# A gated cross-attention and quantised feed-forward kernel: another start, another steady order, five PSUM banks at the end, and first transposes in halves

## What is computed

```
x1  = x + tanh(g_x) * ((ctx @ Wv) @ Wout + bout)
h   = layernorm(layernorm(x1)) * ln1_g + ln1_b
h   = gelu(quant(h) @ ternary(w1).T + b1)             # 256 -> 1024
h   = layernorm(h) * ln2_g + ln2_b
out = x1 + tanh(g_f) * (quant(h) @ ternary(w2).T + b2)  # 1024 -> 256
quant(h)   = round(h * s) / s,  s = 127 / max|h| of the token
ternary(w) = clip(round(w / mean|w|), -1, 1) * mean|w|
```

## Time and profile before

| | |
|---|---|
| median of three runs | 415.7 us |
| profiled execution | 413.45 us |
| its span, first to last instruction | 411.7 us |
| PE, DVE, ACT, POOL busy | 315.3, 299.3, 274.2, 268.2 us |
| mean granted TensorE clock | 0.893 of full |
| bytes moved | 51.56 MB |

### The profile page before, as it was taken

One profiled execution on the slowest core, in us unless ns is written; L12 is line 12 of the kernel. 1 busy time (PEld: TensorE's weight loads), 2 busy tenths in 40 slices (PEclk: granted clock), 3 DMA queues, 4 the chain that ended last, 5 costly groups with the idle time before them and its releaser, 6 DMA issues. The chain is left out here.

```text
span 411.7 us, 5770 instructions
## 1 busy us (share of the span) xinstructions
PE 315.3 (77%) x1661; PEld 201.2 (49%) x1690; DVE 299.3 (73%) x520; ACT 274.2 (67%) x443; POOL 268.2 (65%) x298
## 2 busy tenths in 40 slices
PE   2976827759798989797979797989897666665553
PEld 2855516343556565555555554656464434332232
DVE  0168395978788989797979798979798858565710
ACT  2113672666878887878787888969695959594220
POOL 4052669386878887878787888787777868484100
PEclk9998987997989998989999999989898969695785
DMA  7665213325385756566665657490707161715173
GB/s 236 240 247 191 61 49 83 102 50 130 83 176 121 184 124 158 139 144 139 144 151 131 160 123 178 106 201 28 154 27 153 53 127 52 129 52 103 62 127 94
DMA packets 97974, 51.56 MB, mean 125 GB/s; under 512 B 86567, under 2 KB 88800, under 8 KB 97942
## 3 DMA queue, kind: packets, MB, share of 16 engines
q1 hardware_dynamic: 97046, 51.14, 50.6%
q10 hardware_dynamic: 896, 0.04, 0.1%
HBM read 21.78 MB, written 8.41 MB: 73 GB/s over the span
## 5 line engine op out<-in xcount | busy, mean ns | idle before, releaser
L343 POOL TENSOR_TENSOR y<-u,g_bc 128x1024 f32<-128x1024 f32 x64 | 151.4, 2368 | 41.5 <-ACT u L512 40.9
L681 DVE TENSOR_TENSOR y<-y,slot_c 128x1024 f32<-128x1024 f32 x64 | 77.8, 1216 | 47.3 <-PE slot_c L929 31.5
L968 PE MATMUL bank_f<-w2T,q2T 128*128 128x256 f16 x512 | 78.8, 308 | 9.9 <-DMA q2T<-q 7.6
L685 DVE TENSOR_REDUCE amax<-y 128x1 f32<-128x1024 f32 x64 | 77.6, 1213 | 1.8
L493 ACT ACTIVATE q<-y,scale 128x1024 f16<-128x1024 f32 x64 | 69.9, 1142 | 12.8 <-DMA q2T<-q 9.7
L520 ACT ACTIVATE junk<-u,usum 128x1024 bf16<-128x1024 f32 x64 | 73.5, 1149 | 2.1
L968 PEld LDWEIGHTS bank_f<-w2T,q2T 128*128 128x128 f16 x512 | 55.7, 109 | 29.9 <-issue 10.2
L512 ACT ACTIVATE u<-slot_a,d 128x1024 f32<-128x1024 f32 x32 | 35.4, 1107 | 38.3 <-PE slot_a L957 38.3
L929 PE MATMUL slot_c<-ln_rows,rows 128*128 128x512 bf16 x112 | 41.7, 447 | 16.2 <-ACT rows L503 8.9
L904 PE MATMUL slot_a<-wvo,ctxT 128*128 128x256 f32 x208 | 51.4, 380 | 0.0
L726 DVE SCALAR_TENSOR_TENSOR res<-bank_f,d,x 128x256 f32<-128x256 f32 x64 | 27.8, 476 | 19.2 <-PE bank_f L971 19.2
(11 more groups left out here) (113 smaller groups left out, 449.6 us busy)
## 6 DMA issues: line engine op xcount, KB each, us to landing
c_in<-in_ctx SPq DMA_DIRECT2D x16, 512.0 KB, 5.0
x_in<-in_x SPq DMA_DIRECT2D x16, 512.0 KB, 3.5
out<-res SPq DMA_DIRECT2D x32, 256.0 KB, 2.0
y<-in_L_ffn_w SPq DMA_DIRECT2D x2, 1024.0 KB, 9.1
u<-in_L_xattn_Wkv SPq DMA_DIRECT2D x2, 512.0 KB, 6.2
u<-in_L_xattn_Wout SPq DMA_DIRECT2D x2, 512.0 KB, 7.5
q2T<-q SPq DMA_TRANSPOSE x64, 3.3
g_bc<-in_L_ffn_ln_g SPq DMA_DIRECT2D x1, 512.0 KB, 4.5
```

What stands on the lines that cost most here:

```text
L343: nc.gpsimd.tensor_tensor(y[:, k % 3, t, :], u[:, t, :], g2_bc[:, :], ALU.mult).then_inc(gain2_done, 1)
L681: nc.vector.tensor_tensor(line, line, slot_c[:, :], ALU.add).then_inc(y_done, 1)
L685: nc.vector.tensor_reduce(amax[:, 1, t:t + 1], y[:, k % 3, t, :], AX.X, ALU.max, apply_absolute_value=True).then_inc(amax2_done, 1)
L968: nc.tensor.matmul(acc, q2T[:, t, j, :], w2T[:, j, :], start=(j == 0), stop=False)
```

## The change

The order of the work changes on all engines, and some of the work changes its engine. No tile gets another shape, apart from the transfers named here.

- Start. The attention of set 0 goes to slot_b, that of sets 1 and 2 to bank_q and bank_f. ACT copies wvo before the second half of context 0. DVE sums w1 before the first residual; both raw weights are rounded by ACT in one instruction (`round_weights`); DVE clamps after the copies to f16 instead (`clamp_first`, `clamp_second`; the copy of w2 clamps from above). w2 is summed and scaled in bodies -1 and 0, and its turns stand between the hidden products of set 0. Both halves of attention 1 come in body -2. SP's first loads and turns are written out one by one.
- Steady order. PE: second product 2 of set i-3 goes ahead of the rows, second product 3 to between correction 0 and hidden 0, correction t+1 behind hidden t, second product 0 between correction 2 and hidden 2, second product 1 between the two halves of the attention; one context turn goes to the end of the body before, the other behind hidden 3. ACT makes three quantisations ahead of the GELUs, and the fourth and a context copy behind them. DVE takes finals 2 and 3 right behind row 0. SP issues the transpose of tile 3, then the first transposes, then those of tiles 0 and 1, and puts the context load, the transpose of tile 2 and a store at the end of the body.
- End. `product_bank` gives the second products of sets 14 and 15 places in bank_q, slot_a and slot_b beside bank_f; a product's bias is a function of its own (`second_bias`); bodies 16 and 17 are written out, body 18 is gone; all transposes of sets 14 and 15 stand before the last stores, the last two of which hold one tile each; the scales of set 15 are made for three tiles and for one.
- First transposes. `turn_first` issues two DMA transposes of two tiles each (128 x 512), with semaphores of their own; `hidden(0)` and `hidden(2)` wait for one each, and q1_done counts pairs of tiles.
- d12 gets three buffers instead of two.

The core of the diff:

```diff
@@ SP @@
             def turn_first(k):
 
-                wait(sp, q1_done, k + 1)
-                wait(sp, hid_done, T * k)
-                sp.dma_start_transpose(q1T[:, :, :], q1[:, :, :].rearrange("p t d -> p (t d)")) \
-                    .then_inc(q1T_in, 16)
+                for h in range(2):
+                    two = slice(2 * h, 2 * h + 2)
+                    wait(sp, q1_done, 2 * k + h + 1)
+                    wait(sp, hid_done, T * (k - 1) + 2 * h + 2)
+                    sp.dma_start_transpose(q1T[:, two.start * KD:two.stop * KD, :],
+                                           q1[:, two, :].rearrange("p t d -> p (t d)")) \
+                        .then_inc(q1T_in[h], 16)
...
+            for i in range(2, S):
                 if live(i - 3):
-                    store(i - 3, 0)
-                    turn_second(i - 3, 2)
                     turn_second(i - 3, 3)
                 if live(i):
                     turn_first(i)
...
                 if live(i - 2):
                     turn_second(i - 2, 0)
+                if live(i + 4):
+                    load_x(i + 4)
+                if live(i - 2):
                     turn_second(i - 2, 1)
                 if live(i - 3):
                     store(i - 3, 1)
+                if live(i + 5):
+                    load_context(i + 5)
+                if live(i - 2):
+                    turn_second(i - 2, 2)
+                    store(i - 2, 0)
...
+            turn_second(S - 3, 3)
+            for t in range(T):
+                turn_second(S - 2, t)
+            for t in range(T):
+                turn_second(S - 1, t)
+            store(S - 3, 1)
+            store(S - 2, 0)
+            store(S - 2, 1)
+            store(S - 1, 0)
+            store_tile(S - 1, 2)
+            store_tile(S - 1, 3)
@@ shared @@
+        def product_bank(k, t):
+
+            half = slice(D * (t % 2), D * (t % 2 + 1))
+            if k < S - 2:
+                return bank_f[:, half]
+            if k == S - 2:
+                return bank_q[:, half] if t < 2 else slot_a[:, half]
+            return (slot_a[:, 512:512 + D], slot_a[:, 512 + D:1024], slot_b[:, 0:D],
+                    slot_b[:, 512:512 + D])[t]
@@ ACT @@
+            def round_weights(w):
+
+                line = (w1_raw, w2_raw)[w][:, :, :].rearrange("p k n -> p (k n)")
+                act.wait_ge(wscaled, w + 1)
+                nc.scalar.activation(line, line, ACT.Copy, bias=ROUND, scale=wscale[:, w:w + 1]) \
+                    .then_inc(wrounded, 1)
...
+                if live(i + 3):
+                    take_context(i + 3, 0)
+                if i <= S:
                     take_rows()
                 if live(i - 2):
                     quantise(i - 2, 0)
                     quantise(i - 2, 1)
+                    quantise(i - 2, 2)
...
                     take_context(i + 3, 1)
...
                 if live(i - 2):
-                    quantise(i - 2, 2)
                     quantise(i - 2, 3)
@@ DVE @@
+            def clamp_first(n):
+
+                dve.wait_ge(w1T_copied, n + 1)
+                nc.vector.tensor_scalar(w1T[:, n, :], w1T[:, n, :], 1.0, -1.0, ALU.min, ALU.max) \
+                    .then_inc(w1T_clamped, 1)
...
+                if i == S:
+                    for t in range(T):
+                        row(S - 1, t)
+                        row_max(S - 1, t)
+                        if t == 2:
+                            scales(slice(1, 2), slice(0, 3))
+                    scales(slice(1, 2), slice(3, 4))
+                    final(S - 3, 2)
+                    final(S - 3, 3)
+                    for t in range(T):
+                        final(S - 2, t)
+                    for t in range(T):
+                        final(S - 1, t)
@@ PE, steady order @@
-                if live(i + 3):
-                    turn_context(i + 3, 0)
+                if live(i - 3):
+                    second_product(i - 3, 2)
+                    second_bias(i - 3, 2)
                 if i <= S + 1:
                     turn_rows()
                 if live(i - 1):
                     correction(i - 1, 0)
-                if live(i + 3):
-                    turn_context(i + 3, 1)
                 if live(i - 3):
-                    second_product(i - 3, 2)
+                    second_product(i - 3, 3)
+                    second_bias(i - 3, 3)
+                if live(i):
+                    hidden(0)
                 if live(i - 1):
                     correction(i - 1, 1)
                 if live(i):
-                    hidden(0)
+                    hidden(1)
                 if live(i - 1):
                     correction(i - 1, 2)
+                if live(i - 2):
+                    second_product(i - 2, 0)
+                    second_bias(i - 2, 0)
                 if live(i):
-                    hidden(1)
-                if live(i - 3):
-                    second_product(i - 3, 3)
+                    hidden(2)
                 if live(i - 1):
                     correction(i - 1, 3)
                 if live(i):
-                    hidden(2)
                     hidden(3)
+                if live(i + 3):
+                    turn_context(i + 3, 1)
                 if live(i + 1):
                     shift_first(i + 1)
-                if live(i - 2):
-                    second_product(i - 2, 0)
-                    second_product(i - 2, 1)
                 if live(i + 3):
                     attention(i + 3, 0)
+                if live(i - 2):
+                    second_product(i - 2, 1)
+                    second_bias(i - 2, 1)
+                if live(i + 3):
                     attention(i + 3, 1)
+                if live(i + 4):
+                    turn_context(i + 4, 0)
```

More of the change, by code:

```diff
@@ L522, in square @@
                         .then_inc(square_done, 1)
+                if i == S:
+                    quantise(S - 2, 0)
+                    quantise(S - 2, 1)
+                    take_rows()
+                    quantise(S - 2, 2)
+                    quantise(S - 2, 3)
+                    for t in range(T):
+                        quantise(S - 1, t)
+                    return
+                if i == S + 1:
+                    take_rows()
+                    return
                 if i == -3:
@@ L531, in body @@
                     take_rows()
+                    weight_copy(1)
                     take_context(2, 0)
                     take_context(2, 1)
-                    nc.scalar.activation(table[:, :], half_neg[:, 0, 0:1], ACT.Gelu)
+                    return
+                if i == 0:
+                    for t in range(T):
+                        quantise_first(0, t)
+                    take_rows()
+                    round_weights(1)
+                    for t in range(T):
+                        gelu(t)
+                        square(t)
+                    return
+                if i == 1:
+                    take_context(3, 0)
+                    for t in range(T):
+                        quantise_first(1, t)
+                    take_context(3, 1)
+                    take_rows()
+                    take_context(4, 0)
+                    for t in range(T):
+                        gelu(t)
+                        square(t)
+                    take_context(4, 1)
                     return
@@ L801, in body @@
                 if live(i - 1):
+                    row_max(i - 1, 0)
+                    row(i - 1, 1)
+                    row_max(i - 1, 1)
+                if i == S:
+                    scales(slice(1, 2), slice(0, 2))
+                if live(i - 1):
+                    row(i - 1, 2)
+                    row_max(i - 1, 2)
                     row(i - 1, 3)
```

243 lines of the change are left out of this document (141 added, 102 removed).

## The result

The changed kernel takes 365.34 us (median of four runs, 364.51 to 365.44) against 415.81 (four runs, 414.34 to 417.16): 0.878 of the time, interval 0.875 to 0.8815. The profiled execution took 364.51 with a span of 362.7. The forecast was 373.0, 7.7 more, with 362 to 391 as its range.

The account below looks back on a forecast made before the run. It took one loop per set, from variance through rows and hidden 0 to the GELUs, as the bound, no engine being full. Start -15.2, middle -14.4 and end -13.1 sum to -42.7, from the 415.7 median to 373 us, range 362 to 391.

Parts of the forecast that it names:

- The loop from rows to GELU 0: Steady sets: one loop per set from variance through rows and hidden 0 to the GELUs, no engine full.
- the lower bound: Steady set without a stall: rows at 5.1 and hidden 0 ready at 8.1 us after the variance, 18.1 us a set.
- If power does the same, the scales end at 3.2 instead of 2.35: Steady sets: DVE's scales stall under POOL's power as seen under a multiply, making a set 18.8 us, not 18.1.
- rival (a): Steady sets: no stall beside the power, 18.1 us per set, 8 us less, 365 in all; chance 0.17.
- ran beside nothing before: Steady sets: in the old order DVE's scales overlapped no POOL work; now they start near 1.5 us after the variance.
- Rival (b): Middle: clock drops in most sets or half transposes land late, about 1.2 us a set, 389 in all; chance 0.22.
- I take the whole's values: Split q1T transposes: each half priced like a whole one, 1.28 us to issue and 3.3 to land.
- a tie, no cost: Split q1T transposes: first half lands by 7.4 us after the variance, near when hidden 0 wants it in an 18.8 set.
- -15.2: Start: set 2's first GELU at 83 us against 98.25, by reordered w1 and w2 preparation and earlier attention.
- Rival (d): Start: the lead isn't kept, 8 of the 15 us are lost, 381 in all; chance 0.10.
- -13.1: End: set 15's first GELU to the end takes 39.6 us against 52.7, with transposes before stores and five banks.
- (c): Middle: second product 3 ahead of hidden 0 waits for a late transpose, 22.3 us a set, 418 in all; chance 0.07.

Follow-up runs that it names:

- The probe: Changed kernel plus two unused DVE operations per steady body, 8 columns under POOL's multiply and 512 beside its power: 377.98 us.
- the late-w2 run: Changed kernel with w2's turns behind set 0's hidden products and w2's sum, scale and rounding also later: 372.63 us.
- the run on the kernel before: Kernel before the change, four transposes of each first context half issued twice from set 4 on: 406.28 us against 415.14, ratio 0.978.
- hidden 0 first: Changed kernel, steady bodies: hidden 0 ahead of second product 3, scales ahead of finals 0 and 1, first-half store behind first transposes, among other moves: 369.71 us, ratio 0.890.
- the scales first: Changed kernel with DVE's scales ahead of finals 0 and 1 in the steady bodies: 368.42 us, ratio 0.887.
- The run with the store between: Changed kernel with the store of set 13's second half ahead of set 15's four transposes on SP: 366.58 us.
- the run with both steps: Changed kernel with w2's turns behind set 0's hidden products and 10 useless matmuls in each of bodies 13 to 15: 358.21 us, ratio 0.8635.

## Why the prediction was right, and where it was off

**The bound.** The loop from rows to GELU 0 was the right one to reckon by: with rows at r 5.07, correction 0, second product 3 and hidden 0 put GELU 0 at 8.10, as the lower bound had it (5.1 and 8.1). ACT's three quantisations end there too, where 8.3 was reckoned: the row of GELU 0 shows no wait for PE.

**The steady order.** What failed is one term: "If power does the same, the scales end at 3.2 instead of 2.35". They ended at r 2.27. From the earlier trace rows a stall beside a multiply was carried over to the power, and 18.8 was taken over 18.1; 18.19 was measured, so rival (a), given 0.17, is what the chip did, and its 365 is the time that was measured. Eleven periods of 0.61 less are 6.7 us, all of the miss in the spans. That the total still lay within the range owes something to the range, which had been drawn to hold (a).

The trace of the kernel before already had the answer. The forecast says that the scales "ran beside nothing before". That is so in the set of the earlier trace rows, where they end at 229.22, as the power starts. It isn't so in the sets at 147, 248 and 267 us. POOL first, then DVE:

```profile
147.71 1.67 POOL L326 TENSOR_TENSOR rstd<-var,half_neg 128x8 f32<-128x8 f32 x1
...
147.78 0.15 DVE L707 TENSOR_TENSOR d<-amax_g,deq 128x8 f32<-128x8 f32 x1
```

An operation with two inputs in SBUF starts 0.07 us into the power and takes 0.15 us, and the two behind it, still beside the power, 0.17 and 0.16. This was a row nearer in kind than the earlier trace rows. The probe shows both halves: beside the multiply an 8-column operation is held to its end, beside the power even a 512-column one is not. The rule of the Trainium skill's page "SBUF — State Buffer" (Who interferes with whom), that such pairs exclude each other for the whole instruction, agrees with the multiply here (0.75 us, and 2.12 and 2.21 in the late-w2 run) and not with the power (0.12 to 0.17, and 0.68). By the measurement it must not be used for this power. Why the power lets DVE through, no run tells.

**The clock.** Full clock in the middle was forecast and came (1.00 over the 11 periods with attention, 0.97 over all 13). Rival (b) did not occur. What the clock is worth was not split off in the forecast; the run on the kernel before puts it at 0.70 of the 1.79 per set. In the last passages half clock was forecast, with 19.8 for the first two; 20.05 came, and the run with 10 useless matmuls shows that the clock is the whole of their difference to 18.0.

**DVE nearly the bound.** Forecast 17.6 busy with gaps; 17.39 of 18.08 was seen. It is why hidden 0 first gained nothing; the scales first lost by the transpose of tile 3.

**The halves.** "I take the whole's values": right for the issue (1.22 against 1.28), too long for the landing (2.5 against 3.3). It made no difference, as forecast ("a tie, no cost"); with one whole transfer the total is the same.

**The start.** -15.2 was forecast and -15.2 measured (98.25 to 83.03), but two errors cancel. Set 0 to 1 took 21.18, not 19.2. Of these 2.0, 1.35 are the GELUs, which took 11.55 to the variance at 55.65 where the forecast had 10.2 (to 54.5). It had priced the turns of w2 and of the context between the hidden products at under 1 (44.3 and 9.5 are 53.8), and by the run that moves them they cost about 2, most of it GELU 2's wait of 1.80. The other 0.6 is the way from there, 9.63 where 9.0 was taken; half clock costs it 1.7, so that at full clock it would have been quicker than forecast. Set 1 to 2 took 17.75, not 19.5: no stall, and no second products yet. ACT's rounding of 2048 columns was 2.00 as taken, the f16 clamps 0.38 each for w1 and 0.43 and 0.50 for w2. Rival (d) did not occur: the lead of 15.2 was kept.

**The end.** -13.1 forecast, -13.2 measured; rows at 5.2 from the variance of set 15 (332.86) as forecast, the quantisations start at 15.35 instead of 14.8, the last product ended at 26.0 instead of 26.2. The run with the store between confirms one cause: one store among the transposes costs 2.9 us. The rest of the 13.2 was not taken apart.

**The rival on the other side**, (c), has a real mechanism, and its sign, PE waiting for q2T in the middle, did show in the changed kernel, in small. SP's queue and PE in the set whose variance is at 147.16:

```profile
149.09 1.30 SPq L242 DMA_TRANSPOSE q2T<-q  x1
...
153.79 1.03 PE L1082 MATMUL bank_f<-w2T,q2T 128*128 128x256 f16 x8 [0.91 <-DMA q2T<-q]
```

The transpose of tile 3 was issued at r 1.93, as forecast, and its product started 4.7 us later, 0.91 late. GELU 0 came at r 9.11, and this period is 19.03. In the five sets where PE waited 0.45 to 0.91 us, GELU 0 was 0.13 to 1.01 behind its 8.10, 2.3 us in all; by our estimate the periods without these waits are 17.97, close to the 18.01 of the run with both steps. What delays these landings, no run here tells. The 3.5 us a set of (c) never came.

## What to carry to other kernels

In a loop of several engines, write down the chain from the last-ready value to the first use of the next set, and let only the work that it needs stand between; everything else goes into PE's wait, where it also keeps the clock up. Useless matmuls in a gap can pay, 9 us in the old kernel and 4.6 in the new one, but size them by a measured duration: with twice as many the new one lost 3.5. Before a stall seen beside one instruction is carried over to another, look in the old trace for a place where that other one runs beside the same work; here it was there. Price a DVE operation by what POOL runs beside it, by kind: three tiny operations behind POOL's multiplies took 6.65 us, and all six beside the power 0.9.

## What the runs showed of the hardware

- A DVE operation of 8 columns with two SBUF inputs that starts within a POOL multiply of 1024 columns (2.36 us) ends when the multiply does: it takes 0.62 to 0.91 us when it starts late (14 of the probe), 2.12 and 2.21 when early (the late-w2 run). Beside POOL's power (1.67 us on 8 columns) it runs at its own speed, 0.12 to 0.17 us for 8 columns, started as little as 0.05 us into the power, and 0.68 for 512.
- A DMA transpose of half the columns (512 of 1024) holds the queue nearly as long as a whole one (1.22 against 1.28 us) and lands in 2.5 us instead of 3.1 to 3.3.
- PE's clock decides more than PE's share of busy time suggests: in the passages without attention, at a mean of 0.83 with 14.0 us busy, it cost 2.0 us of 20; with 16.35 us busy and full clock the passage took 18.0. In the old kernel 0.44 us more work a set saved 0.7 us a set.
- An f32 matmul call of 256 columns ran as two instructions of 0.22 us each at full clock.
